# Turning the first norm's rows with VectorE and a round trip through memory in a fused audio tower kernel

## What is computed

```python
h = gelu(x[:, 1:] @ W[:256] + x[:, :1] @ W[256:] + b)          # 16 x 374 x 256
y = layernorm(h)                                               # first norm
sim = (y @ y.T) / max(|y_i| |y_j|, eps)                        # 374 x 374 per batch
h = h + (softmax(sim) @ y + y)                                 # first attention
z = layernorm(h)                                               # second norm
m, r = router(z)                                               # 8 experts, mask and weights per token
q, k, v = (sum_e m_e * (z @ W_e) for W_e in q_proj, k_proj, v_proj)
a = softmax(causal(q @ k.T / sqrt(128))) @ v                   # second attention
out = h + sum_e m_e * r_e * (a @ o_proj_e)
```

## Time and profile before

| | us |
|---|---|
| median of 3 runs | 711.66 (711.36 to 711.82) |
| the profiled execution | 711.77 |
| its span, first to last instruction | 710.1 |

### The profile page before, as it was taken

The page is one execution under the profiler, slowest core; times in us unless marked ns, Lnnn a source line. Parts: engine busy times, 40 slices in busy tenths (PEclk is TensorE's granted clock), DMA queues, the critical chain, the costliest instruction groups (busy, mean ns, idle before and its releaser), DMA issues.

```text
span 710.1 us, 18197 instructions
## 1 busy us (share of the span) xinstructions
PE 705.5 (99%) x5440; PEld 473.1 (67%) x5440; DVE 579.8 (82%) x1455; ACT 378.9 (53%) x808; POOL 400.5 (56%) x655
## 2 busy tenths in 40 slices
PE   9999999999999999999999999999999999999998
PEld 8888666675757666575756666575766657575655
DVE  5788798888879888887979888887988888886736
ACT  4977373554646364563646355464646456364443
POOL 7652325756465566746566575746566674653434
PEclk9999999999999999999999999999999999999999
DMA  9581220202020120202020020202011020201111
GB/s 246 150 188 46 74 45 8 72 3 63 14 63 14 13 65 0 71 7 63 14 55 22 9 68 0 70 8 63 14 23 55 0 71 7 63 17 46 22 68 37
DMA packets 33558, 34.35 MB, mean 48 GB/s; under 512 B 7304, under 2 KB 29304, under 8 KB 33400
## 3 DMA queue, kind: packets, MB, share of 16 engines
q1 hardware_dynamic: 33136, 33.65, 18.4%
q10 hardware_dynamic: 392, 0.32, 0.1%
HBM read 27.70 MB, written 6.26 MB: 48 GB/s over the span
## 4 chain that ended last, share of the span: by engine, by line
PE 98%; issue 1%; POOL 0%; POOLq 0%; DVE 0%; ACT 0%; DVEq 0%
PE bank L1671 76%; PE bank L1734 7%; PE bank L1588 5%; PE bank L1645 3%; PE bank L1577 2%; PE bank L1805 2%; PE bank L1720 1%; PE bank L1783 1%; PE bank L1593 1%; PE bank L1612 1%; PE bank L1756 0%; PE bank L1745 0%; PE bank L1748 0%; POOL region_c L670 0%; POOL region_c L663 0%
## 5 line engine op out<-in xcount | busy, mean ns | idle before, releaser
L1671 PE MATMUL bank<-xm,w_qkv 128*128 128x374 f16 x2304 | 415.7, 322 | 0.0
L1671 PEld LDWEIGHTS bank<-xm,w_qkv 128*128 128x128 f16 x2304 | 220.8, 98 | 139.2
L908 ACT ACTIVATE region_c<-bank,out_w 128x256 f32<-128x256 f32 x180 | 84.8, 471 | 163.2 <-PE bank L1671 162.2
L1274 DVE TENSOR_TENSOR xm<-xT,mask_all 128x1496 f16<-128x1496 f16 x128 | 151.9, 1209 | 0.0
L1671 PE MATMUL bank<-w_o,aoT 128*128 128x512 f16 x540 | 143.3, 379 | 0.0
L1180 DVE SCALAR_TENSOR_TENSOR h<-bank,out_w,h 128x256 f32 (+1 forms) x180 | 86.5, 481 | 48.8 <-ACT region_c L908 43.9
L663 POOL TENSOR_TENSOR region_c<-region_c 128x512 f32<-128x512 f32 x46 | 77.1, 1675 | 27.8 <-ACT region_c L908 22.8
L692 POOL TENSOR_TENSOR exp_hl<-exp,exp_hl 128x128 f16<-128x128 f32 (+2 forms) x48 | 41.9, 875 | 83.7 <-ACT exp_hl L864 83.2
L1671 PEld LDWEIGHTS bank<-w_o,aoT 128*128 128x128 f16 x540 | 50.4, 98 | 39.5
L1159 DVE TENSOR_SCALAR region_b<-h,moments,small 128x256 f32 (+1 forms) x96 | 48.8, 553 | 6.1 <-POOL small L577 6.1
L670 POOL TENSOR_TENSOR region_c<-region_c 128x256 f32<-128x256 f32 x46 | 46.9, 1019 | 8.1 <-POOL region_c L663 7.9
(11 more groups left out here) (200 smaller groups left out, 1067.6 us busy)
## 6 DMA issues: line engine op xcount, KB each, us to landing
mask_all<-d_mask SPq DMA_DIRECT2D x32, 384.0 KB, 3.9
h<-in_x_dram SPq DMA_DIRECT2D x16, 256.0 KB, 5.0
out_dram<-h SPq DMA_DIRECT2D x31, 128.0 KB
rnorm_row<-d_rnorm SPq DMA_DIRECT2D x16, 192.0 KB, 4.1
h<-in_x_dram SPq DMA_DIRECT2D x15, 112.0 KB, 5.4
out_dram<-h SPq DMA_DIRECT2D x15, 112.0 KB
xm<-in_L_ffn_q_proj_dram SPq DMA_DIRECT2D x2, 512.0 KB, 7.5
region_c<-in_L_ffn_k_proj_dram SPq DMA_DIRECT2D x2, 512.0 KB, 6.4
```

Source lines behind the costliest of these rows:

```text
L908: a.activation(prod[:, prod_buf(n, t), q, :], pair_bank(n, p)[:, C:2 * C], ACT.Copy, scale=weights_out(n)[:, t, 2 * q + 1:2 * q + 2]).then ...
L1274: v.tensor_tensor(xm[:, e, :, 0:T], xT[1][:, :, :, 0:T].rearrange("p a c t -> p (a c) t"), mask_all[:, e, 0:T].unsqueeze(1).broadcast_to([ ...
L1671: last = t_.matmul(dst, left[lp], right[rp], start=(starts and k == 0), stop=(stops and k == 2), skip_group_check=True)
```

## The change

For batches 3 to 15 TensorE no longer turns the first norm's rows. VectorE transposes the float32 rows `xs[0]` (128 partitions by 768) in blocks of 32x32, the result is stored to memory, and four loads read it back with the blocks put in their places, in runs of 32 numbers (128 bytes). ScalarE then writes the high part of `xT[0]` from it and VectorE the low part. Batches 0 to 2 are turned as before.

With this come moves. The statistics of batch g1 are taken a step ahead, at the end of the step before, between pairs 6 and 7; `norm_rows(0, g1)` stands first in GpSimd's step; `norm_apply(0, g1)` moves from between the pairs to right behind `residual(f)`, with the block transpose behind it and ahead of `norm_apply(1, f)`; `high(0, g1)` moves ahead of the pairs. The copy of the low probabilities (L1376) moves from VectorE to ScalarE.

```diff
@@ SyncE @@
+            def blocks_out(g):
+                sp.wait_ge(s_blocks_turned, g - BY_BLOCKS + 1).then_inc(s_sp_passed, 1)
+                if after_blocks(g):
+                    sp.wait_ge(s_blocks_loaded, 16 * (P // SQ) * (g - BY_BLOCKS)).then_inc(s_sp_passed, 1)
+                sp.dma_start(d_blocks.rearrange("(p n) -> p n", p=P), blocks).then_inc(s_blocks_stored, 16)
+            def blocks_in(g):
+                sp.wait_ge(s_blocks_stored, 16 * (g - BY_BLOCKS + 1)).then_inc(s_sp_passed, 1)
+                sp.wait_ge(s_lo2, g).then_inc(s_sp_passed, 1)
+                columns = d_blocks.rearrange("(a i k b j) -> b i k a j", a=P // SQ, i=SQ, k=NT * NC, b=P // SQ)
+                for b in range(P // SQ):
+                    sp.dma_start(xs_turned[b * SQ:(b + 1) * SQ, :, :, :].rearrange("p t c (a j) -> p (t c) a j", a=P // SQ),
+                                 columns[b]).then_inc(s_blocks_loaded, 16)
                 if g is not None:
                     norms_out(g)
                     norms_in(g)
+                    if not early(m):
+                        blocks_out(g)
+                        blocks_in(g)
@@ GpSimd, step @@
+                if g1 is not None:
+                    norm_rows(0, g1, 1.0, 1e-38)
                 if n is not None and not final(n):
                     low_probs(n)
                 if f is not None and not early(m):
                     norm_rows(1, f, LN_SCALE ** 4, NORM_EPS * NORM_EPS)
                 if g1 is not None:
-                    norm_rows(0, g1, 1.0, 1e-38)
                     row_scales(g1)
@@ ScalarE @@
+            def turned_high(b):
+                act.wait_ge(s_dots_done, NT * b)
+                act.wait_ge(s_blocks_loaded, 16 * (P // SQ) * (b - BY_BLOCKS + 1))
+                a.activation(xT[0][:, 0, :, :].rearrange("p c (t w) -> p t c w", t=NT), xs_turned[:, :, :, :],
+                             ACT.Copy).then_inc(s_T1_hi, 1)
                         turned_values(n)
+                        turned_probs_low(n)
                         turned_probs(n)
...
                     turned_rows_2(f)
+                    if g1 is not None:
+                        high(0, g1)
...
-                    scale_pairs(5, 7)
+                    scale_pairs(5, 6)
                     if g1 is not None:
-                        high(0, g1)
-                    scale_pairs(7, PAIRS)
-                    if g1 is not None:
-                        turned_rows(g1)
+                        turned_high(g1)
+                    scale_pairs(6, PAIRS)
                     high_v()
@@ VectorE @@
+            def next_norm_stats(b):
+                if following(b) is not None:
+                    dve.wait_ge(s_res_bias1, b + 1).then_inc(s_dve_passed, 1)
+                    norm_stats(0, following(b))
+            def turned_low(b):
+                dve.wait_ge(s_T1_hi, b + 1)
+                v.tensor_tensor(xT[0][:, 1, :, :].rearrange("p c (t w) -> p t c w", t=NT), xs_turned[:, :, :, :],
+                                xT[0][:, 0, :, :].rearrange("p c (t w) -> p t c w", t=NT),
+                                ALU.subtract).then_inc(s_T1_lo, 1)
+            def turn_blocks(b):
+                dve.wait_ge(s_xs1, NT * (b + 1)).then_inc(s_dve_passed, 1)
+                if after_blocks(b):
+                    dve.wait_ge(s_blocks_stored, 16 * (b - BY_BLOCKS)).then_inc(s_dve_passed, 1)
+                v.transpose(blocks, xs[0][:, :, :].rearrange("p t c -> p (t c)")).then_inc(s_blocks_turned, 1)
@@ VectorE, step 1 @@
                     head_low(vT, qkv_bank[2], s_v_hi, m + 1, s_v_lo, qkv_out)
+                    next_norm_stats(g1)
                     return
@@ VectorE, loop step @@
                     residual(f)
-                    turned_probs_low(n)
                     if g1 is not None:
-                        norm_stats(0, g1)
+                        norm_apply(0, g1)
+                        turn_blocks(g1)
                     norm_apply(1, f)
...
                     weight_sum(f)
-                    if g1 is not None:
-                        norm_scaled(0, g1)
-                        norm_apply_tile(0, g1, 0)
                     pairs(5, 6)
                     if g1 is not None:
-                        norm_apply_tile(0, g1, 1)
-                        norm_apply_tile(0, g1, 2)
+                        turned_low(g1)
                     pairs(6, 7)
+                    next_norm_stats(g1)
                     pairs(7, 8)
@@ TensorE @@
             def turn_exp(f):
                 pe.wait_ge(s_exp1_lo, NT * f + NT - 1)
+                if by_blocks(f):
+                    pe.wait_ge(s_mask_row, f)
...
                 if t == first:
+                    if by_blocks(f):
+                        pe.wait_ge(s_lo1, f + 1)
...
-                    pe.wait_ge(s_T1_hi, f + 1)
+                    pe.wait_ge(s_logits_out, f)
                     turn_v(n)
...
                         pair(n, 5 + k)
-                    if g1 is not None:
-                        turn_first(g1)
                     M(23)
```

More of the change, by code:

```diff
@@ L88, in audio_tower_kernel @@
         rnorm_row = sb("rnorm_row", [P, TP])
+        blocks = region_b[:, 2 * NT * C:3 * NT * C]
+        xs_turned = part(region_b, NT * C, NT, NC, P)
         cosine = part(region_a, 0, NT, TP)
@@ L229, in audio_tower_kernel @@
         s_T1_lo = sem("T1_lo")
+        s_blocks_turned = sem("blocks_turned")
+        s_blocks_stored = sem("blocks_stored")
+        s_blocks_loaded = sem("blocks_loaded")
         s_rn_stored = sem("rn_stored")
@@ L329, in pipeline @@
             step(2, 3, 2, 1, 0)
-            with loop_engine.Fori(3, B - 1) as i:
+            with loop_engine.Fori(3, B - 2) as i:
                 step(i, i + 1, i, i - 1, i - 2)
+            step(B - 2, B - 1, B - 2, B - 3, B - 4)
             step(B - 1, None, B - 1, B - 2, B - 3)
@@ L336, in audio_tower_kernel, with by_blocks, following, after_blocks @@
         RP = 8
+        SQ = 32
+        BY_BLOCKS = 3
+        def by_blocks(g):
+            return g is not None and not (isinstance(g, int) and g < BY_BLOCKS)
+        def following(g):
+            return None if g is None or (isinstance(g, int) and g == B - 1) else g + 1
+        def after_blocks(g):
+            return not (isinstance(g, int) and g == BY_BLOCKS)
         def early(m):
@@ L423, in norms_in, with mask_out, mask_in @@
                 sp.dma_start(rnorm_row[:, :], d_rnorm[g, :].partition_broadcast(P)).then_inc(s_rn_loaded, 16)
-            def mask_around(f):
+            def blocks_out(g):
[10 more added lines that the diff above has]
+                                 columns[b]).then_inc(s_blocks_loaded, 16)
+            def mask_out(f):
                 sp.wait_ge(s_mask_row, f + 1).then_inc(s_sp_passed, 1)
                 sp.dma_start(d_mask[f, :].rearrange("(e t) -> e t", e=E), maskT[:, :]).then_inc(s_mask_stored, 16)
+            def mask_in(f):
                 sp.wait_ge(s_mask_stored, 16 * (f + 1)).then_inc(s_sp_passed, 1)
@@ L471, in _ @@
             load_tiles(15)
-            mask_around(0)
+            mask_out(0)
+            mask_in(0)
             def store(n, t):
@@ L504, in step @@
                     load_output_weights()
-                    mask_around(f)
+                    mask_out(f)
+                    mask_in(f)
                 if g is not None:
@@ L886, in turned_values, with turned_probs_low @@
                              as16(turn[0], 2 * NT * D), ACT.Copy).then_inc(s_v_tok_ready, 1)
+            def turned_probs_low(n):
+                if later(n):
+                    act.wait_ge(s_pv_done, n)
+                act.wait_ge(s_pT_lo_turned, n + 1)
+                a.activation(pT[:, 1, :], as16(turn[0], PW), ACT.Copy).then_inc(s_pT_lo, 1)
             def turned_probs(n):
```

9 lines of the change are left out of this document (4 added, 5 removed).

## The result

The changed kernel takes 719.46 us (median, 719.00 to 719.72), the kernel before beside it on the same chip 711.36 (711.27 to 711.82). The ratio is 1.0109, 95% interval 1.0096 to 1.0123: slower by 1.1%. The profiled execution took 719.0 with a span of 717.2, which is 7.1 us more than the 710.1 of before. TensorE's granted clock was full in all slices again.

A forecast was written before the change was run, and what follows sets the result against it. TensorE was taken as the bound, with VectorE at the limit at the step's end. Profiled 711.77 + 1.0 (step 1's statistics) + 4.8 (`turned_low`) = 717.6, median 0.1 lower: 717.5 us; range 706 to 726.

The forecast's parts named there:

- the likeliest case: Whole kernel: the transposes' time is waited away and the step's end gets longer, 717.5 us; chance 0.38.
- part 2: TensorE's wait at `turn_exp`: cover only 0.05 us, so about 0.62 of the 0.67 us saved goes into waiting.
- part 3: Step's end: `turned_low` on VectorE comes second, L670 ends 0.45 us later; 0.4 net in 12 steps, 4.8 us.
- part 5: VectorE ahead of `norm_apply(1, f)`: `norm_apply(0, g1)` 1.06 and block transpose 0.96 us fill freed place, cost nothing.
- part 7: GpSimd's `norm_rows(0, g1)`, ScalarE's low probabilities and `high`, two TensorE waits: all in idle time, cost nothing.
- 8.7 us off TensorE: TensorE: twelve transposes fewer in 13 steps, 13 x 0.67 = 8.7 us, if it never waits more.
- The statistics a step ahead: VectorE, 1.39 us between pairs 6 and 7: free in the loop, 1.0 us once in step 1.
- the block transpose is slow: Rival, VectorE ahead of `norm_apply(1, f)`: transpose up to 1.92 us adds 9 us, 727 in all; chance 0.07.
- The transfers: SyncE's store and four loads: landed at 405 to 407, needed at 409.2, cost nothing.
- VectorE first: Rival, step's end: `turned_low` starts ahead of L663, L670 and all behind 0.8 us later, about 722; chance 0.15.
- The gain arrives: Rival, step's end: L624 or the alternation behind it ends 0.62 us earlier, TensorE keeps all, 703.0; chance 0.18.
- The rule of thumb of the prediction: VectorE and GpSimd excluding one another: whoever comes second ends 0.13 us short of its own length after the first.

The follow-up runs named there:

- experiment 1: Kernel before without TensorE's transposes of the first norm's rows and ScalarE's copies of them for batches 3 to 15: 711.43 us against 711.66.
- experiment 2: Changed kernel without `turned_low`, VectorE's subtraction for the low part of `xT[0]`, for batches 3 to 15: 713.25 us, ratio 1.0020 to the kernel before.
- experiment 10: Kernel before without the first norm's transposes and copies for batches 3 to 15, and expert 5's masked copy moved behind `cosines(f, 1)`: 703.07 us against 711.53.
- experiment 3: Changed kernel with the block transpose moved from ahead of `norm_apply(1, f)` to behind it: 717.73 us, ratio 1.0083 to the kernel before.
- experiment 11: Changed kernel with the store of the turned blocks issued twice, one behind the other, ahead of the loads: 719.46 us, ratio 1.0113 to the kernel before.
- experiment 5: Changed kernel with GpSimd's `low_1` moved from between the sums of tiles 0 and 1 to right behind `row_scales(g1)`: 708.59 us against 711.56 before.
- experiment 6: Changed kernel with the masked copy of expert 5 moved from ahead of `cosines(f, 1)` to behind it: 710.87 us, ratio 0.9992 to the kernel before.
- experiment 8: Changed kernel with `low_1`, expert 5's copy, block transpose and step 1's statistics moved, plus expert 3's masked copy ahead of pair 11's addition: 706.05 us, ratio 0.9920.
- experiment 7: Changed kernel with `low_1` early, expert 5's copy behind `cosines(f, 1)`, block transpose behind `norm_apply(1, f)`, step 1's statistics ahead of `weight_max`: 705.21 us against 711.56.

## Why the prediction was right, and where it was off

The forecast was 717.5, the likeliest case was what happened, and the time is 2.0 us above it. Against the kernel before, the forecast was 5.8 us and the measurement 8.1. The sign and the place rest on parts 2 and 3, which experiments 1 and 2 bear out; two terms put at nothing (parts 5 and 7) were not nothing. By its own parts:

1. *8.7 us off TensorE.* The step of experiment 10 is 40.50 - 0.67 exactly. Right.

2. *The wait swallows it.* Forecast 0.62 of waiting a step ahead of `turn_exp`; experiment 1 has 0.60 to 0.62 and no gain. Right, and it is the part on which the sign hung: by TensorE's busy share alone the answer would have been 703.

3. *`turned_low`, 0.45 later at the end of L670, 0.40 net.* It came second by 0.03 us, ended 0.81 behind L709 (forecast 0.83), and the sum behind it was stretched by 0.50 (forecast 0.45). The two waits that follow from parts 2 and 3 are 0.68 + 0.31 = 0.99 a step, forecast 0.62 + 0.45 = 1.07, so the net at the step's end is 0.32, forecast 0.40. The forecast had it all at `turn_exp` and did not see that `dots(f, 2)` needs a bank that `cosines(f, 0)` frees, ahead of it. Taking `turned_low` out gave 0.52 a step. Right in place and mechanism. That L709 came first was within 0.1 us by the forecast's own rows, and in part luck. The loss is in 11 steps, not 12: the steps that end at `turn_exp` of batches 3 and 15 are 40.43, a little shorter than before. There TensorE stands at `turn_exp` alone, 0.59 us.

4. *The statistics a step ahead.* In the loop they cost nothing, as forecast: the first masked copy behind them (418.98) starts 0.64 before `low_1` ends at 419.62, and ends 0.79 behind it, so GpSimd sets its end and not the statistics. In step 1 they cost 1.08, forecast 1.0, and in the idle time ahead of the router's maximum nothing. Right.

5. *The block transpose, cost nothing.* A mis-sized term: experiment 3 gave 0.21 us a step back, 11 x 0.21 = 2.3 us, about what the forecast's difference of 5.8 lacks to 8.1. The instruction itself is 0.98 (forecast 0.96). From the end of the second norm's statistics to `norm_apply(1, f)` it is 2.42 us (397.79 to 400.21), 1.98 before (393.47 to 395.45), where the forecast had no change. The sum 1.06 + 0.96 has no time for the 0.12 ahead of `norm_apply(0, g1)`, nor for the 0.34 between its end and the block transpose, which reads what it wrote. Less the overlap of the next one that makes 0.44. It did not cost 0.21 alone: the cover of the high part was 0.37 and not 0.2 (it ended at 397.38, TensorE began at 397.81, and in the changed kernel 0.06 lie between the two), and 0.44 would have cost 0.07. The rest is in part 7. The rival "the block transpose is slow" was this same place at another size.

   The sum from the trace is 11 x 0.62 + 1.08 - 2 x 0.07 = 7.8, against 8.1 between the medians; 0.3 stays open. The two spans differ by 7.1, because the prologue of the one execution was 0.67 us ahead of the other's (87.11 against 87.78).

6. *The transfers.* Landed before 408, in a step that begins 4.1 us later than the one of the forecast, so before 404 on its clock; the forecast was 405 to 407. They are needed at 413.47, so with over 5 us of cover; experiment 11 took 2.4 of them away for nothing. Right in what it costs, a little slow in the time.

7. *ScalarE's and GpSimd's moves, nothing.* No wait of TensorE names them, but one was not free. With `norm_rows(0, g1)` first in GpSimd's step, the low part of the probabilities begins 2.02 us behind `turn_exp` (390.46 to 392.48) instead of 1.57 (386.38 to 387.95), and the masked copies of experts 6 and 7 take 2.02 instead of 1.83. The second norm's statistics end 0.24 later behind `turn_exp` than before. With the 0.44 of part 5, the high part ends 0.64 later (11.00 us behind `turn_exp` before, 11.64 now; `norm_apply(1, f)` itself is 0.04 shorter). TensorE is due for it 0.06 later, so it comes 0.58 late against a cover of 0.37: the 0.21. Experiment 3 has the copies at 2.01 and no block transpose ahead, and loses nothing there; experiment 5 has the block transpose in its place and the copies at 1.88, and loses 0.07. So the 0.21 needed both delays. Which of GpSimd's instructions makes the copies wait, no run tested by itself.

Of the two rules of the Trainium skill, the first ("VectorE: DVE Perf Modes", section "The three transpose paths") would have made the block transpose 1.87 us, as an estimate; the trace has 0.98, and the measurement decides. The warning of the same section is of a plain DMA whose innermost destination stride is large. It did not bear on these loads, whose innermost pieces are 128 bytes in a row: 96 KB landed 2.7 us after the issue.

Of the rivals, "VectorE first" failed to happen by 0.03 us in 11 of the 13 steps (by 0.28 in the other two); the forecast's rows could not tell so small a margin. "The gain arrives" named the right place: the alternation behind L624 had to end 0.62 earlier. Experiments 5, 6 and 10 brought that about by other edits, and the gain arrived.

## What to carry to other kernels

Where one engine is busy all the time, ask of each thing that it waits for how much cover the wait has; as long as what it waits for does not become earlier, work taken off the bound engine is worth no more than the smallest cover behind it, even if the profile books no idle time there (with 0.05 us of cover 8.7 us of work were worth nothing). Before such a change, move what can be moved out of the chain that becomes the next bound: that costs nothing while the first bound holds and decides the worth of the change (711.43 and 711.62 alone, 703.07 together). When VectorE and GpSimd exclude one another, count the order of their starts as well as their durations, and run an order again after every edit: in experiment 8 an earlier start of GpSimd turned a race, and the copies behind it ended 0.8 us later.

Two delays that each lie near a cover add up. The block transpose lost 0.07 us a step when the copies ahead of it were short (experiment 5), the longer copies lost nothing without it (experiment 3), and together they lost 0.21.

## What the runs showed of the hardware

- The rule of thumb of the prediction held for the pairs shown here: the one of VectorE and GpSimd that comes second ends about 0.13 to 0.15 us short of its own length after the first has ended (`turned_low` 0.81 behind L709 with a length of 0.96; the copy of expert 5 0.79 behind L723 with 0.92). The Trainium skill has this on "SBUF — State Buffer", section "SBUF: two separate sides": the shared port pair is an exclusive lock that whoever starts first holds for the whole instruction. The rows agree, and they show the price over the whole kernel: 15.6 us of VectorE's busy time and 23.5 of GpSimd's between experiment 7 and the changed kernel, for the same instructions.
- A GpSimd instruction that waits gets in between two VectorE instructions that stand back to back: L738 comes at 385.55, under the first copy, and the pair of copies takes 2.47 us instead of 1.84 (experiment 8). Two long copies in a row are no protection.
- The block transpose reads what `norm_apply(0, g1)` ahead of it on VectorE wrote, and starts 0.34 us behind its end (L1246 behind L1226), with two waits of VectorE between them. Independent ones overlap by 0.08 (L1226 at 400.21, ahead of the end of L1246 at 400.29). No run shows how much of the 0.34 is due to the second wait.
- VectorE's block transpose of 128x768 float32 took 0.98 us, as long as a subtraction with two inputs of that shape (L1329, 0.96).
